# Placing the routed tokens behind the first maximum in the steps with few scan turns

## Time and profile before

| | |
|---|---|
| median of 3 runs | 1869.99 us |
| profiled execution | 1867.18 us, its span 1865.5 us |
| mean granted TensorE clock | 0.854 of full |
| busy over the span | PE 71%, DVE 67%, POOL 54%, ACT 46% |
| positions, steps 5 to 12 | L1261 at 720, 779, 837, 893, 938, 980, 1013, 1035 us |
| positions, steps 16 to 23 | L1261 at 1134, 1168, 1202, 1236, 1267, 1298, 1326, 1344 us |

### The profile page before, as it was taken

The page is one execution under the profiler, slowest core; times in us unless marked ns, Lnnn a source line. Parts: engine busy times, 40 slices in busy tenths (PEclk is TensorE's granted clock), DMA queues, the critical chain, the costliest instruction groups (busy, mean ns, idle before and its releaser), DMA issues. The chain is left out here.

```text
span 1865.5 us, 32852 instructions
## 1 busy us (share of the span) xinstructions
PE 1325.9 (71%) x9000; PEld 1151.7 (62%) x9001; DVE 1254.0 (67%) x3301; ACT 849.6 (46%) x2808; POOL 1000.8 (54%) x1234
## 2 busy tenths in 40 slices
PE   6277106850036676766765899998489999999997
PEld 4265105630025465654654778876389999999997
DVE  3798999999988999999876144454434444443442
ACT  5433213442113665667766488887322322322332
POOL 3367868987669999998866324342111122122121
PEclk9689558885568878878877999998789999999999
DMA  5344001566031010100002111133130410411200
GB/s 139 74 102 111 12 6 42 143 173 95 23 120 38 23 33 18 32 27 27 28 27 84 57 42 52 54 120 120 40 103 21 154 48 22 158 42 45 77 17 7
DMA packets 182719, 119.29 MB, mean 64 GB/s; under 512 B 124849, under 2 KB 163560, under 8 KB 182120
## 3 DMA queue, kind: packets, MB, share of 16 engines
q1 hardware_dynamic: 119848, 90.98, 17.4%
q10 hardware_dynamic: 58864, 18.71, 4.0%
q0 software_dynamic: 3920, 8.60, 1.3%
HBM read 83.44 MB, written 35.74 MB: 64 GB/s over the span
## 5 line engine op out<-in xcount | busy, mean ns | idle before, releaser
L246 POOL TENSOR_TENSOR wt<-wt 128x1024 f32<-128x1024 f32 x128 | 301.5, 2355 | 53.9 <-DVE wt L191 46.9
L252 POOL TENSOR_TENSOR wt<-wt 128x512 f32<-128x512 f32 (+2 forms) x384 | 307.6, 801 | 30.1
L1942 PE MATMUL e_ph<-e_g,e_w 128*128 128x128 f32 x2496 | 285.2, 275 | 0.7 <-ACT e_g L1912 0.7
L1942 PEld LDWEIGHTS e_ph<-e_g,e_w 128*128 128x128 f32 x2496 | 281.9, 192 | 0.9 <-issue 0.9
L191 DVE SCALAR_TENSOR_TENSOR wt<-wt,scan 128x256 f32<-128x256 f32 x512 | 242.0, 473 | 18.0 <-POOL wt L246 13.4
L170 DVE TENSOR_REDUCE wt<-wt 128x16 f32<-128x272 f32 x512 | 219.2, 428 | 0.1
L181 DVE TENSOR_TENSOR scan<-wt,scan 128x256 f32<-128x256 f32 x512 | 215.0, 420 | 0.3
L159 DVE TENSOR_TENSOR wt<-wt,scan 128x256 f32<-128x256 f32 x512 | 210.1, 410 | 0.9 <-PEq L269 0.5
L1420 ACT ACTIVATE wt<-p_pX,p_mx 128x120 f32<-128x120 f32 x512 | 176.4, 387 | 71.9 <-DVE p_mx L1205 70.3
L1903 ACT ACTIVATE e_g<-e_ph,wt 128x128 f32<-128x128 f32 x156 | 48.7, 363 | 304.9 <-PE e_ph L1942 304.9
L1821 POOL TENSOR_TENSOR e_ve<-e_mv,eps 128x1 f32<-128x1 f32 x39 | 7.4, 190 | 327.1 <-DVE e_mv L1877 327.1
(11 more groups left out here) (226 smaller groups left out, 2925.0 us busy)
## 6 DMA issues: line engine op xcount, KB each, us to landing
wt<-in_L_ffn_W SPq DMA_DIRECT2D x24, 1024.0 KB
qkv<-f_st ACTq DMA_DIRECT2D x48, 256.0 KB, 2.6
p_kE<-kE SPq DMA_DIRECT2D x16, 480.0 KB, 3.7
p_vP<-vP SPq DMA_DIRECT2D x16, 480.0 KB
wt<-qkv SPq DMA_DIRECT2D x12, 512.0 KB, 6.4
e_xt<-routed ACTq DMA_DIRECT2D x39, 130.0 KB, 2.1
f_xt<-in_x SPq DMA_DIRECT2D x32, 128.0 KB, 2.8
p_oT<-o SPq DMA_DIRECT2D x16, 256.0 KB
```

Source lines behind the costliest of these rows:

```text
L246: nc.gpsimd.tensor_tensor(x, s["S"][:, h, z * Q:(z + 1) * Q], s["qn"][:, h, z * Q:(z + 1) * Q].rearrange("p t (o d) -> p t o d", o=1).to_b ...
L252: nc.gpsimd.tensor_tensor(x[:, :, :, 0:half], x[:, :, :, 0:half], x[:, :, :, half:2 * half], ALU.add).then_inc(s["o_fold"][h], 1)
L1942: ins = nc.tensor.matmul(ph2[:, c // 2, c % 2], w2[:, s, i, c * P:(c + 1) * P], g1[:, i], start=(i == 0), stop=(i == C1 - 1))
```

## The change

In the steps with fewer than 16 scan turns, `positions(e)` is called behind `maximum(c, 0)` and `scan(4)`, and not ahead of `maximum(c, 0)`. The other engines' programs are as they were.

```diff
                 scan(2)
                 scan(3)
-                if "e" in on:
+                few = len(turns) < 2 * R
+                if "e" in on and not few:
                     positions(e)
                 if "c" in on:
                     maximum(c, 0)
                 scan(4)
+                if "e" in on and few:
+                    positions(e)
                 if "c" in on:
                     maximum(c, 1)
                 scan(5)
```

## The result

| | before | after |
|---|---|---|
| median of the runs compared | 1866.5 us (5 runs, 1863.3 to 1873.3) | 1882.4 us (5 runs, 1878.6 to 1884.6) |
| profiled execution | 1867.18 us | 1884.62 us |

The kernel is slower: after stands to before as 1.0077, with an interval of 1.0052 to 1.0102. The forecast, 1884.6 against 1870.0 us, is a ratio of 1.0078. The profiled execution of after happens to be the slowest of its five, so its distance to before (17.4 us) is above the 14.4 us that the ratio gives (0.0077 x 1866.5). The two medians are 15.9 us apart, which lies inside the interval of the ratio too. The forecast's range for the time after was 1874 to 1889 us. One execution of the kernel before, in the last rounds, took 2456.7 us at a granted clock of 0.548 and is left out of every ratio.

A forecast was written before the change was run, and what follows sets the result against it. No single engine was taken to bound step 8, a chain across engines sets it; TensorE bounds step 16. 7.6 + 3.4 + 0.6 + 3.0 = 14.6 us more gave 1884.6 us against 1869.99, range 1874 to 1889.

The forecast's parts named there:

- Down(f, 0) held: Steps 8 and 9: TensorE's down(f, 0) waits for the later positions and starts 3.8 us later, 7.6 us together.
- No slack behind it: Steps 8 and 9: the delay passes whole through mlp_out, statistics, second_norm and queries into the next step, 3.8 us each.
- the covered case: Rival, 16%: other work ends last in steps 8 and 9, so the hole is covered; 4.8 us more, 1874.8 us.
- The sign given for it: Evidence against cover in step 8: VectorE's mlp_out starts 0.06 us after down(f, 1) ends.
- The slow clock: Steps 8 and 9: TensorE's clock falls in the hole before down(f, 0), +1.7 us each, 3.4 together; bounds 0 and 1.85.
- Step 10, 0.6: Step 10: maximum 1 comes behind positions and delays ScalarE and GpSimd, +0.6 us; bounds 0 and 0.7.
- Send hidden: Steps 8 and 9: GpSimd's later send costs nothing; in step 9 10.98 us of idle time covers 4 us.
- Steps 16 to 20, 0.6 each: Steps without scan: down(f, 0) starts 0.7 us later, costing 0.6 us a step, 3.0 together; bounds 0.3 and 0.7.
- the clock that does not fall: Rival, 14%: TensorE's clock stays up in the two holes of steps 8 and 9; 11.2 us more, 1881.2 us.
- the clock that comes back elsewhere: Rival, 6%: half-clock passes in steps 8 to 10 and 20 to 23 recover 1.8 us each; 1870.4 us, not slower.
- the slow clock in the small holes: Rival, 6%: slow passes also follow the 0.7 us holes of steps 16 to 20, adding 8.3 us; 1892.9 us.
- the spared no-scan steps: Rival, 8%: the steps without scan are not slowed; 11.6 us more, 1881.6 us.

The follow-up runs named there:

- fill of the holes: Changed kernel plus 14, or in a second kernel 7, unused TensorE matmuls before the held down(f, 0) in steps 8 and 9: ratios 1.0071 and 1.0063 against before.
- early half: Kernel before with positions moved only in steps 8 to 10, steps 16 to 21 left as they were: 1882.5 us, ratio 1.0073.
- one turn more: Kernel before with positions moved only in steps 8 to 10, one scan turn further than the change, behind maximum 1: 1888.7 us, ratio 1.0117.
- late half: Kernel before with positions moved only in the steps without scan turns, 16 to 21: 1873.7 us, ratio 1.0015.

## Why the prediction was right

- **Down(f, 0) held, 3.8 us a step: right.** From count to the pass 6.79 us in step 8 (899.75 - 892.96), and 3.18 before (895.99 - 892.81): 3.6. Step 9 gives 6.80 - 3.18 = 3.6. The 0.2 us are the distance from positions' first instruction to the pass: 0.27 and not the 0.42 of the earlier trace rows.
- **No slack behind it: right.** Mlp_out +6.6, second_norm +6.6, queries +6.6 (each with the 0.15 by which step 8 starts later); the covered case would have shown less at some link. The sign given for it was weaker than it looked: before, VectorE was busy until mlp_out (a reciprocal, L1212, at 904.43) and did not wait for down(f, 1) there, both were merely ready at the same moment. After, it waits 1.46 us.
- **The slow clock, 1.7 us a step: the mechanism right, the size too small.** The pass takes 5.39 us to the start of values, for 2.79 before, which is 2.6; values are still slow in their first part (2.12 for 1.88), 0.24. Together 2.8 us in step 8 and 3.0 in step 9 (2.60 + 0.36). By the fill of the holes it is 2.0 to 2.2 a step on average, so the size is known only as 2 to 3 us. The pass was to be 4.4 to 4.5 us long and is 5.46. My upper bound of 1.85 was what half clock costs the queries, 3.7 us for 1.9; but the pass here is 2.8 long at full clock, so half clock throughout costs it 2.8. I had the row for that the earlier trace rows and took the price of a hole of 1.65 us, after which the full clock came back within the pass. By these rows two steps cost 5.8 us, 2.4 more than forecast.
- The rule of the Trainium skill ("TensorE: Matmul & The Clock Gate", "Part 1: The HAM clock gate") that I weighed would have let the term vanish in one step. It did not. In the profiles of after, of its early half and of the kernel with one turn more, all six holes of steps 8 and 9 are followed by a slow pass (4.98 to 5.46 us). Where the rule's variation does show is in steps 5 to 7, which all these kernels share: in after the slow passes are those of steps 5 and 6 (4.51 and 4.46 us, behind 1.59 and 1.75), in the early half that of step 7 alone (4.39, behind 1.82), in the one with a turn more that of step 6 alone. It costs nothing there, since VectorE sets the pace. It shows on the chain too: the gate passes behind second_norm in step 8 run at full clock in after and in part at half in the early half and three more of the kernels that hold down(f, 0) there (one turn more, 14 and 7 matmuls).
- **Step 10, 0.6: right in after** (0.52), which is partly luck: in the five other kernels that move positions in step 10 it loses 1.1 to 1.4 us, of which step 11 gives back 0.4 to 0.6. **Send hidden: right** (4.87 and 13.44 us of idle time).
- **Steps 16 to 20, 0.6 each: right in three, low in two.** 0.55, 0.53, 0.51, 0.78, 0.80 are 3.2 us for 3.0. Step 22's 0.45 us is not the change's: 17.0 to 18.0 us occur there with and without it (17.57 with the late half alone, 18.02 in the kernel before with unused matmuls).
- **The sum.** 7.2 + 5.8 + 0.5 + 3.2 = 16.7 by the profile's parts (of 17.5 from count to count; 0.2 us in each of steps 8 and 9 lie in the passes just behind the queries, the rest in steps 11 to 15, 21 and 22), 14.6 forecast, 14.4 measured by the ratio with 9.7 to 19.0 as its interval. The hit to 0.1 per thousand is luck, while the mechanism and the steps are not: the two large terms erred, by -0.4 and +2.4, and the measurement can't tell 14.6 from 16.7.

The rivals: the clock that does not fall is refuted by 0.50 in the pass, the covered hole by second_norm, the clock that comes back elsewhere by the queries (3.75 us, as before; it did come back in the gate and up passes from 915.22 on, which take 3.7 us for 5.4, but TensorE then waits 3.95 us for second_norm where it waited 0.90, so nothing is won), the slow clock in the small holes by 2.83 us behind 0.73, and the spared no-scan steps by their 0.5 to 0.8 us each.

## To carry to other kernels

Where an in-order queue holds an instruction that another engine waits for, look at what stands behind the wait on that other engine, not at what it gets out of the way of: here a move by one scan turn bought nothing and held a pass by all of 3.6 us. A hole opened in TensorE's stream on the critical chain is paid twice, once for itself and once for the matmuls behind it at the lower clock (here 2 to 3 us behind 3.5 us of idle time, nothing behind 0.7 us); a hole of 1.6 to 1.8 us, with a slow pass behind it, costs nothing where another engine is busy for 98% of the step. And where such holes are already on the chain, a few unused matmuls that end before the awaited data come can win more than reordering (0.8% here), while too many cost nearly as much as the change did.

## What the runs showed of the hardware that was not expected

- An fp32 matmul of 128 x 128 by 128 x 256 stands in the trace as two rows of 0.23 us each: 14 of them are x28 and 6.31 us.
- Behind the four holes of 3.5 us, in after and in the early half, the lower clock lasted for nearly the whole pass (5.3 to 5.5 us) and in three of them into the next operation (2.2 to 2.3 us for 2.0); behind 7.5 us the pass was no slower (5.11 and 4.98).
- Filling a hole does not settle the clock of the rest of the step: with 7 matmuls in the hole of step 8, the transposes and the gate pass 26 us later ran at 0.51 (1.04 and 1.92 us for 0.66 and 1.03), as they did with the hole open in the early half, and did not in after.
- The start of step 5, ahead of which all these kernels are alike, lies between 709.7 and 717.7 us in the fourteen profiled executions. That alone moves a single time by up to 8 us, more than half of the effect studied; distances from count to count don't contain it.
